# One core, an attention with a recurrence woven into it: the recurrent layer's stages are taken up at other half iterations

## The reference, cut to what matters

```python
x = _L0_xattn_ref(x, ctx_2048, ...)
x = _L1_xattn_ref(x, ctx_2048, mask_Bx1xSxS2_ff0, ...)
x = _L2_xattn_ref(ctx_2048, x, mask_BxS2_ik0, ...)
x = _L3_xattn_ref(x, ctx_2048, ...)
...
# layer 3, per token
a = k_t[..., :, None] * v_t[..., None, :]
out = jnp.einsum('bhi,bhij->bhj', r_t, u * a + s)
s = a + w_t[..., :, None] * s
...
x1 = x + og * g @ Wo.T
rr = jax.nn.sigmoid(xr2 @ Wfr.T)
kk = jnp.square(jax.nn.relu(xk2 @ Wfk.T))
return x1 + rr * (kk @ Wfv.T)
```

## Time and profile before

| | |
|---|---|
| median of three executions | 1898.7 us (1892.6 to 1900.48) |
| profiled execution | 1900.49 us, of which span 1898.4 us |
| PE, DVE, ACT, POOL busy | 1644.6, 1216.3, 895.3, 819.3 us |
| mean granted TensorE clock | 0.934 |
| blocks 1 to 7, start to start | 224.1, 222.0, 221.4, 226.7, 224.4, 221.4, 228.1 us |
| block 0 before them, last block behind them | 191.7, 138.6 us |

### The profile page before, as it was taken

One profiled execution on the slowest core, in us unless ns is written; L12 is line 12 of the kernel. 1 busy time (PEld: TensorE's weight loads), 2 busy tenths in 40 slices (PEclk: granted clock), 3 DMA queues, 4 the chain that ended last, 5 costly groups with the idle time before them and its releaser, 6 DMA issues.

```text
span 1898.4 us, 34750 instructions
## 1 busy us (share of the span) xinstructions
PE 1644.6 (87%) x13615; PEld 1026.3 (54%) x13615; DVE 1216.3 (64%) x2121; ACT 895.3 (47%) x1855; POOL 819.3 (43%) x903
## 2 busy tenths in 40 slices
PE   5888998899997898898987999979998889889726
PEld 3665555565574655555554655646556465556203
DVE  4752578656886468844786457864688546873483
ACT  4453554445554545545554456444455544553202
POOL 5631248404573147702494035831467114860080
PEclk8998898999999999999988989899999999899857
DMA  6001014200421005100141102410052001410070
GB/s 185 1 2 36 1 23 56 43 19 1 50 38 34 19 1 69 25 28 19 21 55 30 35 1 33 54 35 18 1 63 30 28 19 11 59 24 13 2 88 12
DMA packets 73568, 60.79 MB, mean 32 GB/s; under 512 B 38960, under 2 KB 56512, under 8 KB 73408
## 3 DMA queue, kind: packets, MB, share of 16 engines
q1 hardware_dynamic: 55648, 47.99, 17.3%
q10 hardware_dynamic: 17216, 10.55, 2.0%
q0 software_dynamic: 544, 0.03, 0.0%
HBM read 20.28 MB, written 4.19 MB: 13 GB/s over the span
## 4 chain that ended last, share of the span: by engine, by line
PE 66%; DVE 14%; ACT 8%; POOL 6%; issue 4%; DMA 0%; DVEq 0%; SPq 0%; POOLq 0%; ACTq 0%
PE bank L638 26%; PE bank L777 8%; PE bank L1019 6%; DVE late L1305 6%; PE bank L957 5%; PE bank L654 4%; PE bank L982 3%; PE bank L717 2%; POOL soft_ring L1670 2%; PE bank L910 2%; POOL late L1625 2%; ACT soft_ring L1149 2%; DVE late L1317 2%; PE bank L975 1%; PE bank L886 1%
## 5 line engine op out<-in xcount | busy, mean ns | idle before, releaser
L1670 POOL TENSOR_TENSOR soft_ring<-soft_ring,seg_max 128x512 f32<-128x512 f32 x256 | 283.0, 1120 | 307.9 <-DVE seg_max L1467 307.2
L1305 DVE TENSOR_TENSOR_SCAN late<-late 128x520 f32<-128x520 f32 x128 | 232.2, 1814 | 16.8 <-POOL late L1627 12.4
L1164 ACT ACTIVATE soft_ring<-soft_ring 128x512 f32<-128x512 f32 x256 | 160.0, 625 | 172.3 <-POOL soft_ring L1670 172.3
L1625 POOL TENSOR_TENSOR late<-late 128x520 f32<-128x520 f32 x128 | 197.2, 1541 | 72.3 <-DVE late L1359 53.1
L777 PE MATMUL bank<-early 32*128 32x128 f32 (+2 forms) x1024 | 153.0, 417 | 37.9 <-ACT soft_ring L1149 35.1
L957 PE MATMUL bank<-ident,soft_ring 128*128 128x128 f32 x1024 | 166.3, 292 | 21.9 <-ACT soft_ring L1164 19.1
L957 PEld LDWEIGHTS bank<-ident,soft_ring 128*128 128x128 f32 x1024 | 116.2, 146 | 103.6 <-issue 53.8
L1467 DVE TENSOR_REDUCE seg_max<-soft_ring 128x8 f32<-128x512 f32 (+1 forms) x256 | 166.6, 675 | 0.2
L1678 POOL TENSOR_SCALAR soft_ring<-soft_ring,rden 128x256 f32<-128x256 f32 x64 | 65.5, 1023 | 214.9 <-DVE rden L1429 214.9
L1047 ACT ACTIVATE late<-bank 128x512 f32<-128x512 f32 (+2 forms) x104 | 60.5, 596 | 158.4 <-PE bank L638 158.2
L638 PE MATMUL bank<-early,w 128*128 128x512 f32 x256 | 120.7, 622 | 15.9 <-ACT early L1221 15.9
(11 more groups left out here) (255 smaller groups left out, 3281.4 us busy)
## 6 DMA issues: line engine op xcount, KB each, us to landing
late<-late SPq DMA_DIRECT2D x128, 260.0 KB, 4.4
c<-in_ctx ACTq DMA_DIRECT2D x8, 512.0 KB, 4.0
x<-in_x ACTq DMA_DIRECT2D x8, 512.0 KB, 4.9
out_x<-late SPq DMA_DIRECT2D x8, 512.0 KB, 2.9
mask<-in_mask_Bx1xSxS_ff ACTq DMA_DIRECT2D x16, 128.0 KB, 4.0
mask<-in_mask_BxS_ik SPq DMA_DIRECT2D x8, 256.0 KB, 3.3
w<-in_L_xattn_mlp_w SPq DMA_DIRECT2D x2, 1024.0 KB, 8.7
wkv<-in_L_xattn_kv_w SPq DMA_DIRECT2D x1, 512.0 KB, 4.1
```

The lines of the kernel that those rows point to most:

```text
L1164: af(soft[:, u % SOFT, :], soft[:, u % SOFT, :], ACT.Exp).then_inc(sig("exp"), 1)
L1305: nc.vector.tensor_tensor_scan(sj[:, n % 2, :], wP[:, k, :, :].rearrange("p b t -> p (b t)"), aj[:, n % 2, :], 0.0, ALU.mult, ALU.add).the ...
L1625: tt(aj[:, n % 2, :], kP[:, k, :, :].rearrange("p b t -> p (b t)"), vj[:, n % 3, :], ALU.mult).then_inc(sig("kv_done"), 1)
L1670: tt(s, s, seg_max[:, u % SOFT, 0:segs].unsqueeze(2).broadcast_to([128, segs, 512 // segs]), ALU.subtract).then_inc(sig("sub"), 1)
```

## The change

The two tables get other numbers: 28 of the 29 stages and all 19 rounds have at least one engine whose half iteration differs. Nothing else is edited: no instruction is added or removed in the source, and SP's queue is the same. Shown are some of the lines; the others are of the same kind.

```diff
-            "shift": (14, 16, 12, 2),
-            "maa": (16, 16, 12, 7),
+            "shift": (13, 14, 10, 3),
+            "maa": (15, 16, 13, 3),
...
-            "mix 2": (35, 33, 35, 19),
+            "mix 2": (36, 34, 33, 20),
...
-            "turn 2": (130, 129, 125, 128),
-            "shift 2": (132, 133, 128, 132),
-            "ffn k": (133, 133, 129, 132),
-            "ffn r": (133, 133, 132, 132),
-            "ffn v": (134, 133, 134, 132),
+            "turn 2": (133, 132, 133, 129),
+            "shift 2": (138, 132, 134, 133),
+            "ffn k": (142, 134, 139, 138),
+            "ffn r": (144, 137, 139, 141),
+            "ffn v": (144, 137, 139, 142),
...
-            (65, 51, 64, 63), (70, 54, 67, 63), (70, 54, 67, 63), (71, 66, 67, 64), (73, 69, 67, 64),
+            (73, 56, 65, 65), (74, 59, 69, 67), (74, 70, 69, 67), (74, 73, 69, 67), (77, 73, 69, 67),
```

More of the change, by code:

```diff
@@ L459, in build @@
             "moments": (0, 0, 0, 0),
-            "normalize": (3, 10, 1, 1),
-            "turn": (11, 11, 5, 1),
-            "shift": (14, 16, 12, 2),
-            "maa": (16, 16, 12, 7),
[L464 to L467, removed]
-            "mix 2": (35, 33, 35, 19),
[L469 to L482, removed]
-            "turn 2": (130, 129, 125, 128),
-            "shift 2": (132, 133, 128, 132),
-            "ffn k": (133, 133, 129, 132),
-            "ffn r": (133, 133, 132, 132),
-            "ffn v": (134, 133, 134, 132),
+            "normalize": (8, 5, 1, 2),
+            "turn": (11, 12, 5, 2),
+            "shift": (13, 14, 10, 3),
+            "maa": (15, 16, 13, 3),
+            "mix 0": (18, 25, 19, 10),
+            "mix 1": (22, 28, 27, 10),
+            "td": (28, 33, 30, 10),
+            "k": (34, 33, 33, 12),
+            "mix 2": (36, 34, 33, 20),
+            "decay": (37, 37, 37, 20),
+            "v": (42, 39, 39, 20),
+            "mix 3": (43, 41, 41, 33),
+            "mix 4": (46, 43, 43, 44),
+            "r": (48, 45, 44, 49),
+            "g": (48, 45, 47, 49),
+            "r u k": (52, 51, 48, 49),
+            "bonus": (54, 56, 57, 56),
+            "center": (125, 122, 121, 122),
+            "variance": (125, 122, 126, 122),
+            "gate": (126, 122, 127, 122),
+            "project": (127, 128, 131, 123),
+            "moments 2": (128, 130, 131, 127),
+            "normalize 2": (131, 130, 132, 129),
+            "turn 2": (133, 132, 133, 129),
[3 more added lines that the diff above has]
+            "ffn v": (144, 137, 139, 142),
         }
         SCAN_PLACES = (
[4 rows of a table removed]
[4 rows of a table added]
         )
```

## The result

| | before | changed |
|---|---|---|
| median, range | 1896.1 us (1892.6 to 1900.48, 4 runs) | 1914.9 us (1911.62 to 1921.46, 4 runs) |
| profiled execution, its span | 1900.49, 1898.4 us | 1911.62, 1909.6 us |
| mean granted clock | 0.934 | 0.935 |

The ratio is 1.0095 with a 95% interval of 1.0065 to 1.0125: the change made the kernel 0.95% slower, where I forecast +1.0 us with 0.46 for no change, 0.30 for slower. The loss is clear of the noise. The time lies inside my range of 8 in 10 (1883 to 1916) only near its end, in the part that was there for a rival; the forecast's own range (1891 to 1909) and its "within 0.5%" miss it.

The account below looks back on a forecast made before the run. PE was taken to bound each block, so only its waits and clock could change. Terms 8.0 - 4.9 - 3.5 + 1.0 + 0.4 = +1.0 us on 1898.7, rounded to 1900 us; 8-in-10 range 1883 to 1916.

Parts of the forecast that it names:

- The first sum: Recurrence's start: PE's sum behind layer 2's first scores delays DVE's read and masks; +8.0 us, bounds 0 and 22.
- The delay of DVE falls into those waits: Block 4's recurrence start: PE's existing waits absorb DVE's delay, second transposition within 0.4 us of before.
- The two kinds of block: First-sum loss by block: 2.5 us in blocks 3 and 6, 2.0 in block 2, 0.25 in 1, 4, 5, 7.
- The normalization ahead of scan 0: DVE at the recurrence's start: normalizing before scanning shortens PE's wait; gain 0.6 us, between 0 and 1.3.
- DVE is ready for the read at about 745.2 + 0.6: Read of round 4 in block 3: scan 0 behind the normalization makes DVE ready only 0.6 us later.
- The gain of 0.8: Normalization at the recurrence's start: by the shared-port lock rule, the gain would be 0.8 us in place of 0.6.
- The clock: Rival, chance 0.30 including more of the stall: PE's longer wait before layer 2's second scores lowers its clock; 1912 us.
- If all seven blocks run DVE's chain at the low clock: Slower rival's condition: scores 1.1 us and projection 1.0 us later, +13 us in all, 1912 us.
- The feed-forward block: Turn 2 and layer 3's last products: PE's 0.76 us wait goes; -0.7 us a block, -4.9 us.
- The end of the recurrence: Earlier scan 10 on DVE starts the products sooner, PE's 2.43 us wait shrinks; -0.5 us a block, -3.5 us.
- Layer 0 and iterations 9 to 23: Layer 0: one PE wait shrinks, a 0.9 us one appears, +0.15 a block; iterations 9 to 23: no PE wait.
- if the blocks differ from before by more than 1.3 us on average: Sign that the forecast is wrong, read from the lengths of blocks 1 to 7, expected at 222 to 226 us.

Follow-up runs that it names:

- E5: Kernel before with one number changed: scan 0 on DVE from 64 to 65, behind the normalization; 1910.4 us, ratio 1.0078.
- E3: Changed kernel with PE's first sum (scan 4) put back from 77 to 73, the second sum left late; 1899.3 us, ratio 1.0006.
- E7: Changed kernel with PE's first sum, DVE's scan 0 and POOL's scans 0 to 7 put back, second sum left late; 1896.6 us, ratio 1.0004.
- E8: Changed kernel with 6 extra products, results unread, behind the first sum in PE's wait; 1903.0 us, ratio 1.0030.
- E10: Kernel before with extra products, results unread, in five of PE's waits; 1885.7 us, ratio 0.9953.
- E11: Changed kernel with extra unread products in PE's waits, 6 of them behind the first sum; 1903.4 us, ratio 1.0035.
- E2: Kernel before with both PE sums late: scan 4 from 73 to 77, scan 6 from 76 to 80; 1912.7 us, ratio 1.0080.
- E6: Kernel before with only PE's second sum (scan 6) late, from 76 to 80; 1899.8 us, ratio 1.0000.
- E1: Changed kernel with both PE sums put back, scan 4 at 73 and scan 6 at 76; 1907.6 us, ratio 1.0060.
- E12: Changed kernel with the recurrence's start put back and extra unread products in PE's waits, none at half iteration 80; 1892.8 us, ratio 0.9992.
- E9: Kernel before with only the change's second half, scans 10 to 18 and center to ffn v on all engines; 1894.7 us, ratio 0.9995.

## Why the prediction was right or wrong

*The first sum.* The mechanism was right: the sum runs behind the scores, DVE's read waits for it, the masks are late, PE waits 4 to 5 us (4.9 to 5.5). PE's second scores start 3.0 us later in the block on average (115.8 against 112.8), my 3.1. But DVE's read waits 0.81 us in three blocks and 1.95 to 2.50 in the others, where I had 2.9 in one kind of block and 1.2 in the other: a part of the delay is the later rounds, the next part's. The term was mis-sized: +8.0 us against 7 x 2.83 = 20 (my sum had the 0.6 of the next part in it). The step that failed is "The delay of DVE falls into those waits", by which I gave blocks 1, 4, 5 and 7 0.25 us each. The second turn came later by 1.8, 1.8, 2.7 and 3.7 us there, measured from the first. The wait that was to take the delay up, 2.2 to 2.7 us before L957, was taken by slow products. The two kinds of block were no fixed property: the same block is of one kind in one kernel and of the other in the next.

*The normalization ahead of scan 0.* Wrong in sign, and in a step I hardly argued: "DVE is ready for the read at about 745.2 + 0.6". I looked at who waits for the normalization and not at who waits for the scan. POOL's product of the third round needs the scan's buffer; it waits 1.43 us, and since POOL's product and copy and DVE's scan and read follow each other without a pause, 2.83 us a round, the rounds never catch up. E5 prices it at 0.78% in the order of before, but that price does not stand in the changed kernel: E3, which keeps this edit and takes the first sum back, is at 1.0006, E7, which takes both back, at 1.0004. The costs do not add up; with the second sum behind the projection the late rounds cost nothing that the time shows.

The gain itself was there and was lost to another edit. In E5 PE's wait before the first turn fell by 0.9 us, to 0.54. In the changed kernel it is 1.67: the pair of L1489 takes 1.94 us where it takes 1.13 in E5 and took 1.62 before. Beside it runs POOL's L1702 until 735.34, and the pair ends at 735.49; in E5 L1702 is elsewhere. That L1702 is what holds it up is my reading of these rows; no run moves it alone. The rule of the Trainium skill that I weighed (SBUF - State Buffer, Who interferes with whom) fits these rows: POOL's product, 2.21 us beside the scan, takes 1.28 when the scan is behind it. The gain of 0.8 that I worked out by it came in E5 (0.9) and not in the changed kernel.

*The clock.* What I carried as a rival (0.30, 1912 us, "If all seven blocks run DVE's chain at the low clock") is what happened, near its size: the median is 1914.9. E8 shows it: with the wait filled, 0.65% came back. E10 and E11 divide the loss from turn to turn. In blocks without slow products it is 26.3 us in the order of before and 28.0 in the changed one, so 1.7 us a block are the order alone. The clock makes the rest: before it added 0.7 on average (27.05), in the changed kernel 1.8 (29.88). Of the 2.83 us, then, 1.7 are waiting and 1.1 the clock, an estimate, since the filled kernels differ in more than the clock. Over the whole kernel there is no more slow work than before: PE's busy time (1641.4 and 1644.6 us) and the mean clock (0.935 and 0.934) are the same. It stands at another place, behind a wait that nothing fills. So my rival came near the time, but its picture, slow work added to that of before, is not what the sums show. The Trainium skill (TensorE: Matmul & The Clock Gate, HAM oscillation) says that idle gaps bring the clock down; the rows agree, 2.07 against 1.16 us for the same products. E2 and E5 each cost nearly the whole loss alone and together only a little more, and E3 and E6 cost nothing. In E1 and E5 the scores that follow the projection take 2.08 us in all seven blocks, in the kernel before in five, in E3 in none. That fits, but what decides on slow work is not shown by the length of the wait alone: behind 2.4 us the second scores were fast in all blocks of E6 and E12, behind 2.2 slow in two of E3.

*The feed-forward block.* The wait of 0.76 us is gone and ffn k does not wait for shift 2, as forecast. A new one of 0.27 us stands before ffn v. Measured -0.47 a block, forecast -0.7. It is the same 0.47 between the undisturbed blocks (50.31 and 49.84), so this gain is the order's.

*The end of the recurrence.* Forecast -0.5, measured -0.35 and -0.13 ahead of it in one profile; E9 gives nothing in the time, and the shortest blocks are equal (13.57 and 13.55), so in an undisturbed block the order gains nothing here. PE's wait is 3.11 us in block 3, not 2: what I gained on DVE came back as waiting on PE.

*Layer 0 and iterations 9 to 23.* Right: the wait of 1.11 us fell to 0.19, and one of 0.81 came behind it for what is drained late (forecast 0.9). The start of iteration 9 moved by -0.13 us (forecast +0.15). No wait in iterations 9 to 23. The last block is 0.4 us longer, as forecast.

Of my tests, "if the blocks differ from before by more than 1.3 us on average" has come true (1.7), and the longest of the blocks takes 230.9 us where I had 226 as the bound.

Open: which blocks run slow behind a wait, and why E5 has more of them far from its edit; the 8 us of the loss that the profiles do not hold; and how much of the loss is DVE's reads. In block 3 of the changed kernel the read of round 4 takes 1.16 us beside POOL's L1625 and that of round 5 1.15 beside L1697; both take 0.66 to 0.69 in E1, E2 and E5. E9 gains nothing in the time although its span is 3.4 us shorter; here too the profiled execution of before lay 4.4 us above its median (E9's 2.4 above its own).

## What to carry to other kernels

When an instruction is moved ahead of another, follow both: who waits for the one that comes later now, on every engine and through every ring of buffers. A chain that alternates between two engines at their full pace does not make up a delay at its head. Ask also what else is queued on the other engines: a gain that came alone was lost when POOL's order moved too. Compare profiles only with a look at where each lies among its kernel's runs. And a wait of PE is not priced by its length: put independent work of PE into a wait rather than beside full stretches. That waits should not be gathered into one piece is what E12 suggests; it was not tested alone.

## What I had not expected of the hardware

Useless products made a kernel faster: 6 of 0.77 us in a wait of 5.5 us gave back 12 us of 1915 in seven blocks, and ten a block in five waits took 0.47% off the kernel before. Its 35 runs lay between 1887.5 and 1906.1 us, the 12 with the extra products between 1884.6 and 1889.4. The mean granted clock does not tell the two first kernels apart: it is 0.935 in the changed one and 0.934 in the one before. The granted clock of a short stretch and the lengths of equal products behind a wait do.
